# Routing by the graph's chunks of 125 rows, five of them added and normalised beside the last half hop

## What is computed

```python
    xn = _layernorm(x, axis=-1)
    x = x + _L0_gnn_ref(xn, ...) + _L0_mix_ref(xn[None], ...)[0]
    x = x + _L0_ffn_ref(_layernorm(x, axis=-1)[None], ...)[0]
    xn = _layernorm(x, axis=-1)
    x = x + _L1_gnn_ref(xn, ...) + _L1_mix_ref(xn[None], ...)[0]
    x = x + _L1_ffn_ref(_layernorm(x, axis=-1)[None], ...)[0]
```

```python
        for kk in range(NUM_K):
            gnn_out = gnn_out + _graph_gcn(gnn_out, row, col, gate_w[kk], gate_b[kk], n_nodes)
        return jnp.concatenate([x1, gnn_out], axis=1)
```

```python
        router_logits = jnp.einsum('bsh,he->bse', x, gate)
        routing_weights, selected = jax.lax.top_k(router_logits, TOP_K)
        routing_weights = jax.nn.softmax(routing_weights, axis=-1)
        ...
        out = jnp.einsum('ebsh,bse->bsh', eo, tok_w)
```

## Time and profile before

| | |
|---|---|
| median of 3 runs | 2486.34 us (2482.85 to 2488.85) |
| the profiled execution | 2485.95 us |
| its span (first to last instruction) | 2484.2 us |
| mean granted clock of TensorE | 0.945 |
| busy: TensorE / its weight loads / VectorE | 91% / 80% / 63% |
| busy: ScalarE / POOL | 40% / 10% |

### The profile page before, as it was taken

The page is one execution under the profiler, slowest core; times in us unless marked ns, Lnnn a source line. Parts: engine busy times, 40 slices in busy tenths (PEclk is TensorE's granted clock), DMA queues, the critical chain, the costliest instruction groups (busy, mean ns, idle before and its releaser), DMA issues. The chain is left out here.

```text
span 2484.2 us, 33706 instructions
## 1 busy us (share of the span) xinstructions
PE 2249.1 (91%) x12632; PEld 1984.6 (80%) x12632; DVE 1575.5 (63%) x2626; ACT 997.1 (40%) x1552; POOL 252.2 (10%) x262
## 2 busy tenths in 40 slices
PE   6889999996977999966999999958989999989898
PEld 4679999995866778765888888847789999978697
DVE  7646665568867888765899999957623333245422
ACT  4122232226744454413888888851121212221120
POOL 0057773000000000011000000011000000000000
PEclk9989999998997999956999999979999999999899
DMA  4332221114438345076445645134312111224314
GB/s 171 121 90 43 48 70 40 39 47 146 155 124 317 121 197 212 21 281 247 153 153 190 234 175 182 60 144 163 112 45 74 39 39 41 83 96 146 110 44 140
DMA packets 117152, 305.10 MB, mean 123 GB/s; under 512 B 18794, under 2 KB 45794, under 8 KB 116986
## 3 DMA queue, kind: packets, MB, share of 16 engines
q1 hardware_dynamic: 106170, 281.93, 32.0%
q0 software_dynamic: 10816, 20.99, 3.0%
HBM read 297.82 MB, written 126.51 MB: 171 GB/s over the span
## 5 line engine op out<-in xcount | busy, mean ns | idle before, releaser
L2255 DVE TENSOR_TENSOR ex_wl<-exraw,ex_wh 128x1024 fp32r<-128x1024 f32 x324 | 375.6, 1218 | 21.2 <-ACT ex_wh L2322 20.5
L2322 ACT ACTIVATE ex_wh<-exraw 128x1024 fp32r<-128x1024 f32 x324 | 328.5, 1057 | 49.3 <-DMA exraw<-in_experts 18.5
L1517 DVE TENSOR_TENSOR m_kvf<-m_bank,m_bkv 128x256 f32<-128x256 f32 (+1 forms) x160 | 67.9, 424 | 221.4 <-PE m_bank L1422 221.4
L1183 POOL DMA_INDIRECT scratch_slots<-pay,idx x160 | 197.8, 1236 | 57.5 <-issue 57.5
L1422 PE MATMUL m_bank<-m_w_lo,xh 128*128 128x256 f32 (+1 forms) x1280 | 178.3, 281 | 0.0
L1422 PE MATMUL m_bank<-m_w_hi,xl 128*128 128x256 f32 (+1 forms) x1280 | 177.0, 280 | 0.0
L1422 PE MATMUL m_bank<-m_w_hi,xh 128*128 128x256 f32 (+1 forms) x1280 | 176.9, 281 | 0.0
L1691 PE MATMUL gl_bank<-gl_gh,gl_al 125*125 125x512 f32 x400 | 159.1, 398 | 8.0 <-DVE gl_al L1859 8.0
L1422 PEld LDWEIGHTS m_bank<-m_w_lo,xh 128*128 128x128 f32 (+1 forms) x1280 | 163.9, 186 | 0.1
L1422 PEld LDWEIGHTS m_bank<-m_w_hi,xl 128*128 128x128 f32 (+1 forms) x1280 | 162.3, 186 | 0.0
L1422 PEld LDWEIGHTS m_bank<-m_w_hi,xh 128*128 128x128 f32 (+1 forms) x1280 | 161.4, 186 | 0.0
(11 more groups left out here) (437 smaller groups left out, 5159.4 us busy)
## 6 DMA issues: line engine op xcount, KB each, us to landing
exraw<-in_experts SPq DMA_DIRECT2D x328, 512.0 KB
scratch_seats<-raw SPq DMA_DIRECT2D x95, 512.0 KB
raw<-in_qkv SPq DMA_DIRECT2D x48, 512.0 KB, 5.6
xr<-scratch_res SPq DMA_DIRECT2D x42, 512.0 KB, 3.6
scratch_res<-xr SPq DMA_DIRECT2D x40, 512.0 KB, 3.9
xr<-scratch_seats SPq DMA_DIRECT2D x27, 512.0 KB, 3.7
scratch_served<-ex_y SPq DMA_DIRECT2D x27, 512.0 KB, 2.6
scratch_at<-xr SPq DMA_DIRECT2D x48, 209.0 KB, 1.9
```

Source lines behind the costliest of these rows:

```text
L1183: e.indirect_dma_start(dram["slot_rows"], bass.IndirectOffsetOnAxis(idx[:, k:k + 1].bitcast(U32), 0), pay[:, k, :], None).then_inc(scat.se ...
L1517: e.tensor_tensor(f, bank[KVB + s % 3][0:r, 0:W2], bkv[0:r], ALU.add)
L2255: return e.tensor_tensor(wl[:, n % RING], raw[:, unit[1]], wh[:, n % RING].bitcast(F32), ALU.subtract)
L2322: e.activation(wh[:, n % RING], raw[:, unit[1]], ACT.Copy).then_inc(high.sem)
```

## The change

- **Hops.** `graph_layer` gets the residual and its chunks' buffers (`rows`, `xn`). In the second hop SyncE loads eight chunks of 125 residual rows. The last half hop has no dots, bias, halving and spreads. VectorE takes in their place three `moments_of` (the addition of `g` to the residual's upper half, and moments) at steps 3, 5 and 7, two more and all five scalings after the loop. TensorE does the last `JOINT` = 3 steps bank by bank, so that the banks end one after another (`ended`). SyncE stores the five early chunks' sums to `res` and loads the residual's chunks 8 and 9 behind the first two. `x2` is gone: the result stays in `g`. `half` shares memory with `th` and `af`.
- **Routing** works on the ten chunks of 125. The first five come normalised; the last five are added and normalised here. The gate is SyncE's first transfer, the experts' four first units follow. On TensorE the order is turn(c+1), a ranking where c+1 is 5, 6, 7 or 9, scoring(c). `valid` and some memsets are gone. `Norm` takes its chunks, its rows and its depth of buffers.
- **Serving** works on the chunks of 125 too; its loads and stores go through `move`, two transfers each in place of one. The experts' unit buffers `exraw` are a list, half of which (`last`) lives from the graph's phase on.

```diff
+    def __init__(self, p, chunks=range(TC), rows=rows_of, depth=2):
...
+    HOPS, HALF, RING, LATE, JOINT = 4, TC // 2, 4, 2, 3
...
+        EARLY = T[:HALF]
+        norm = Norm(p, EARLY, node_rows, HALF)
+        x_in = [p.raises(f"x_in{c}", [c], 32) for c in T]
...
+        thaf = p.sb("thaf", [P, 6, HALF * TP])
+        th, af = thaf[:, 0:2], thaf[:, 2:6]
+        half = flat(thaf[:]).bitcast(U16)[:, 0:HALF * N].rearrange("p (c n) -> p c n", n=N)
...
+                if k == 1:
+                    for t in res_stored:
+                        e.wait_ge(*t.last())
+                    for c in T[:2 * HALF - 2]:
+                        move(e, rows[c], res[nodes(c)], x_in[c].sem)
                 for i in blanks[k * len(blanks) // HOPS:(k + 1) * len(blanks) // HOPS]:
                     e.dma_start(seats[i * P:(i + 1) * P], zero).then_inc(blanked.sem, 16)
             e.wait_ge(*blanked[blanks[-1]])
-            e.wait_ge(*rest_out[HOPS - 1, 1])
-            for c in T[:HALF]:
-                move(e, dram["x2"][nodes(c)], g[:, c], stored[c].sem)
-            for c in T[HALF:]:
-                e.wait_ge(*last_out[c])
-                move(e, dram["x2"][nodes(c)], g[:, c], stored[c].sem)
+            for c in EARLY:
+                e.wait_ge(*added[c])
+                move(e, res[nodes(c)], rows[c], x_out[c].sem)
+                if c == 2:
+                    for f, l in ((0, TC - 2), (1, TC - 1)):
+                        e.wait_ge(*x_out[f][f])
+                        e.wait_ge(*scaled[f])
+                        move(e, rows[l], res[nodes(l)], x_in[l].sem)
...
+                    joint = T[-JOINT:] if (k, h) == halves[-1] else T[TC:]
+                    for c in T[:TC - len(joint)]:
...
+                    for d in range(HALF) if joint else ():
+                        for c in joint:
+                            if d == 0:
+                                e.wait_ge(*a_low[k, h, c])
+                            b, cut = nth[k, h, c] % RING, slice(d * TP, d * TP + TP)
+                            o = bank[BANKS[h][d]][0:TP, :]
+                            e.matmul(o, al[0:TP, b, cut], gh[0:TP, c], start=False, stop=False)
+                            e.matmul(o, ah[0:TP, b, cut], gl[0:TP, c], start=False, stop=False)
+                            m = e.matmul(o, ah[0:TP, b, cut], gh[0:TP, c], start=False, stop=c == TC - 1)
+                        m.then_inc(ended.sem)
...
+                    if (k, h) != halves[-1]:
+                        copy_row(1 - h, (k, 1 - h))
+            for c in EARLY:
+                norm.root(e, c)
...
+            def moments_of(c):
+                t = rows[c][0:TP, NH:D]
+                e.wait_ge(*x_in[c][c])
+                e.tensor_tensor(t, t, g[0:TP, c], ALU.add).then_inc(added.sem)
+                e.drain()
+                norm.moments_of(e, rows[c][0:TP], c)
+
+            def scale(c):
+                norm.scale(e, xn[c][0:TP], rows[c][0:TP], c).then_inc(scaled.sem)
...
+                elif (k, half) == (0, halves[-1]):
+                    if s in (LATE + 1, LATE + 3, LATE + 5):
+                        moments_of((s - LATE - 1) // 2)
...
-            e.wait_ge(*a_done[HOPS - 1, 1, TC - 1])
+            moments_of(3)
+            scale(0)
+            moments_of(4)
+            scale(1)
             for d in range(HALF):
-                update(1, [d]).then_inc(last_out.sem)
-
-        p.hand_on(*stored)
-    return stored
+                e.wait_ge(*ended[d])
+                update(1, [d])
+                if d + 2 < HALF:
+                    scale(d + 2)
+
+        p.hand_on(*x_in[HALF:], *x_out)
+    return x_in[HALF:], x_out
...
-            def load(c):
-                if c >= BUFS:
-                    e.wait_ge(*x_out[c % BUFS][c - BUFS])
-                    e.wait_ge(*normed[c - BUFS])
-                e.dma_start(row(c), res[tokens(c)]).then_inc(x_in[c % BUFS].sem, 16)
-                for b in range(TC):
-                    if c * P < (b + 1) * TP and b * TP < c * P + rows_of(c):
-                        e.wait_ge(*x2_stored[b][b])
-                e.dma_start(xg[0:rows_of(c), c % BUFS], x2[tokens(c)]).then_inc(x_in[c % BUFS].sem, 16)
...
-            for c in range(BUFS):
-                load(c)
-                if c == 1:
-                    e.dma_start(flat(gr[:]), gate_dram).then_inc(ld.sem, 16)
-            for c in C:
+            e.dma_start(flat(gr[:]), gate_dram).then_inc(ld.sem, 16)
+            for u in range(FIRST):
+                e.dma_start(exraw[u], w_dram[u]).then_inc(units_in.sem, 16)
+            for c in C[H:]:
                 e.wait_ge(*added[c])
-                e.dma_start(res[tokens(c)], row(c)).then_inc(x_out[c % BUFS].sem, 16)
-                if c + BUFS < TC:
-                    load(c + BUFS)
-                else:
-                    for u in range(c - BUFS, min(c - BUFS + 1, FIRST)):
-                        e.dma_start(exraw[:, u], w_dram[u]).then_inc(units_in.sem, 16)
-            for b in range(KEPT, BUFS):
-                e.wait_ge(*x_out[b][TC - BUFS + b])
+                move(e, res[nodes(c)], rows[c], x_out[c - H].sem)
...
             for c in C:
-                r = rows_of(c)
                 if c % 2 == 0:
                     e.wait_ge(*seated[c // 2])
                 for k in range(TOP):
-                    e.indirect_dma_start(seats, bass.IndirectOffsetOnAxis(seat[0:r, k, c:c + 1].bitcast(U32), 0),
-                                         xn[0:r, c], None).then_inc(scattered.sem, 16)
+                    e.indirect_dma_start(seats, bass.IndirectOffsetOnAxis(seat[:, k, c:c + 1].bitcast(U32), 0),
+                                         xn(c), None).then_inc(scattered.sem, 16)
             e.wait_ge(*scattered[TC - 1, TOP - 1])
...
+                if c >= H:
+                    e.wait_ge(*normed[c])
...
-                if c >= 3 and c % 2:
-                    rank(c // 2 - 1)
+                b = c % 2
                 if c + 1 < TC:
                     turn(c + 1)
+                if c + 1 in (H, H + 1, H + 2, H + 4):
+                    rank((0, 1, 2, 3, 3)[c + 1 - H])
...
+                e.wait_ge(*x_in[c - H][c])
+                t = rows[c][0:TP, NH:D]
+                e.tensor_tensor(t, t, g[0:TP, c], ALU.add).then_inc(added.sem)
                 d()
...
-                    e.tensor_tensor(sel[:, pair], sel[:, pair], valid[:, pair].unsqueeze(2).broadcast_to([P, 2, EX]),
-                                    ALU.mult).then_inc(chosen.sem)
+                e.tensor_tensor(sel[:, pair], hot[:, 0, pair], hot[:, 1, pair], ALU.add).then_inc(chosen.sem)
...
-            moments_of(0)
-            for c in C:
-                r = rows_of(c)
+            moments_of(H)
+            for c in C[H:]:
                 if c + 1 < TC:
                     moments_of(c + 1)
-                n.scale(e, xn[0:r, c], row(c), c).then_inc(normed.sem)
-                if c >= 3 and c % 2:
-                    choose(c // 2 - 1)
-                if c >= 4 and c % 2 == 0:
-                    give(c // 2 - 2)
+                n.scale(e, xn(c), rows[c][0:TP], c).then_inc(normed.sem)
+                if c > H and c + 1 < TC:
+                    give(c - H - 1)
+                if c + 2 < TC:
+                    choose(c - H)
+            choose(PAIRS[-2])
...
-                e.dma_start(xr[0:rows_of(c), c % 3], res[tokens(c)]).then_inc(x_in[c % 3].sem, 16)
+                move(e, xr[:, c % 3], res[nodes(c)], x_in[c % 3].sem)
...
-                e.dma_start(res[tokens(c)], xr[0:rows_of(c), c % 3]).then_inc(x_out[c % 3].sem, 16)
+                move(e, res[nodes(c)], xr[:, c % 3], x_out[c % 3].sem)
...
+            with sb("g", [P, TC, NH]) as g, sb("exlast", [P, UNITS - FIRST, D]) as last:
+                rows = [xr[:, 0], xr[:, 1], xr[:, 2], raw[:, 1], raw[:, 2], last[:, 5], last[:, 6], last[:, 7],
+                        xr[:, 0], xr[:, 1]]
+                early = [last[:, c] for c in range(TC // 2)]
...
+                with sb("exfirst", [P, FIRST, D]) as begin:
+                    exraw = [begin[:, u] for u in range(FIRST)] + [last[:, u] for u in range(UNITS - FIRST)]
```

More of the change, by code:

```diff
@@ L1592, in graph_layer @@
         blank, blanked = p.raises("blank", ["zero"]), p.raises("blanked", blanks, 16)
[L1593 to L1594 removed]
+        EARLY = T[:HALF]
+        norm = Norm(p, EARLY, node_rows, HALF)
+        x_in = [p.raises(f"x_in{c}", [c], 32) for c in T]
+        added, scaled, x_out = p.raises("added", EARLY), p.raises("scaled", EARLY), [p.raises(f"x_out{c}", [c], 32) for c in EARLY]
+        p.take(*res_stored)
         gh, gl = p.sb("gh", [P, TC, NH], F32R), p.sb("gl", [P, TC, NH], F32R)
@@ L1887, with route @@
 FIRST = 4
-def route(nc, tag, x2, res, gate_dram, seats, seat, answer, share, plan, x2_stored, res_stored, xr, w_dram, exraw):
+def route(nc, tag, g, res, gate_dram, seats, seat, answer, share, plan, rows, early, x_in, w_dram, exraw):
     with Phase(nc, tag) as p:
-        C, U = range(TC), range(KC)
```

(37 more changed lines are left out.)

181 lines of the change are left out of this document (79 added, 102 removed).

## The result

The changed kernel takes 2499.76 us (median of 5 runs, 2494.92 to 2504.17), the kernel before 2487.46 (5 runs, 2482.85 to 2489.11): a ratio of 1.005, 95% interval 1.0031 to 1.007. It is **slower by 0.5%**, where 2475.7 us and a faster kernel were forecast; the time lies above the stated range of 2468 to 2483. On another chip it was 1.004 (1.0024 to 1.0056).

What follows compares the result with a forecast made beforehand. Phases add up; TensorE bounds routing, and VectorE would end the graph's phase. The terms -13.9 - 0.2 + 0.4 + 1.9 + 1.2 = -10.6 us take 2485.95 to 2475.3, median 2475.7; range 2468 to 2483.

Steps and rivals of the forecast that it cites:

- The bound and the first part of the sum: Graph's end through routing: VectorE ends the graph's phase, TensorE bounds routing; last choice at 1120.5 instead of 1134.4, 13.9 us gained.
- First turn: Start of routing: the gate, now issued first, lands after 3.0 us, so TensorE's first turn comes at 1062.5.
- Ten turns, scorings and rankings: TensorE in routing: ten turns, ten scorings and four rankings take 57.6 us, plus 0.4 before the last choice.
- The three moments in the loop: Graph's last half hop: three moments, 8.2 us, lie inside VectorE's loop, which it leaves at 1042.0 instead of 1042.1.
- Scatters and gathers of 125 rows: Routing's end and serving's start: slower landings add 0.4 us at the last scatter and 1.9 before the first mixing.
- The second case: Five engines, in turn: 125-row transfers use five engines, three fly at once; 1.8 us over the forecast, 2477.5; chance 0.32.
- the third case: Scatters always on the same five engines can't overlap, taking 81 us; about 2513, slower than before; chance 0.04.
- Small items: Serving: a second store issue 0.4, 27 more rows 0.2, waits and semaphore clears 0.6, together +1.2 us.
- the clock rises: Routing: TensorE's work halves at a higher clock, VectorE sets the pace, the time is 2454; chance 0.08.
- A clock above 0.50: Routing: turns and scorings were expected without gaps at granted clock 0.50; a higher clock would show the forecast wrong.

Runs made afterwards that it cites:

- sc120: The changed kernel with scatters of 120 rows, five rows of each chunk not brought to the experts, gathers as they were: 2483.13 us, run once.
- pad_no_joint_2: Second run of the kernel padded to 128 rows with the last three steps' products step by step and updates behind the last product: 2475.36 us.
- pad_sc127: The changed kernel with gathers padded to 128 rows but scatters of 127 rows: 2583.04 us, one run on a slower chip.
- pad_both: The padded kernel: the changed kernel with every scatter and gather padded from 125 to 128 rows: 2472.78 us, ratio 0.9949 to the kernel before.
- pad_uncut: The kernel padded to 128 rows, with serving's residual loads as one 128-row transfer instead of 112 + 13: 2468.65 us, ratio 0.994 to the kernel before.

## Why the prediction was wrong, point by point

- **The bound and the first part of the sum: right.** Forecast: a graph's phase of 323.0 us (736.5 to 1059.5); measured 322.8. VectorE, not TensorE, ends it, 4 us behind the last product, and undoing the bank order costs what that says. First turn: forecast 3.0 us behind routing's start, measured 1.7. Ten turns, scorings and rankings: forecast 58.0 us, measured 55.8 with the clock up for a moment and 58.7 or 58.8 in two traces (`sc120`, `pad_no_joint_2`) where it stayed at 0.50; in the third such trace, `pad_sc127`, it was 60.1. Together 17.6 us gained up to the last choice, 13.9 forecast, and some 3 of the 17.6 are the clock's, which the forecast did not have. (The three moments in the loop stand at steps 5, 7 and 9 counted from 0, not at 3, 5 and 7; VectorE left the loop 305.2 us into the phase, 305.5 forecast.)
- **The step that failed: "Scatters and gathers of 125 rows".** It took the 98-row landing of the earlier trace rows as the measure, scaled its excess to 1.9 us, and charged +0.4 for the scatters' tail and +1.9 for the first gather. Measured: +13.4 and +9.7 against before, 23.1 us where 2.3 were forecast; 11.4 and 8.5 by the padded kernel on one chip. Of the sum's terms this one alone turned a gain into a loss: all the others together measured -13.3 against -12.9 forecast, and that they agree so well is luck, as a larger computing gain and 5.5 us of scatter ahead of the graph's phase offset what serving and the phases behind it lost. 98 divides by 14; no number from 6 to 16 divides 125. The nearest row in bytes was the wrong neighbour: it lay on the other side of the rule.
- **The second case had the mechanism and a wrong price.** "Five engines, in turn" forecast a landing of 6.3 us; the first scatter took 7.0. What failed is its next sentence, "three can fly at once". The second scatter is issued 1.54 us behind the first, but in the packet records nothing of it starts earlier than 3.9 us behind the first one's first packet (about 1.5 us with 128 rows). Later scatters do overlap, and not all on the same five engines: from 1120 to 1130 the queue moves 234 GB/s, nearly twice 5/16 of 404. Yet it is not 404, though the share is 0.92: a packet of 4096 bytes takes 0.249 us in the mean of the twenty scatters against 0.169 in `pad_both`, with medians of 0.159 and 0.162. So the landings grow from 7.0 to 18.0, and the last packet ends 17.7 us behind the last issue (3.7 in `pad_both`). The truth lies between the second and the third case. I had priced the second at 1.8 us over the forecast.
- **What the second and third case left out.** The landing of a single scatter on an idle queue does not tell what a queue costs that is fed faster than it drains. The rival that ended slower had the right question (does a scatter cost more than the interval between issues?) and I set its chance at 0.04.
- **Small items: +1.2 forecast.** Measured +6.2 in the rest of serving and +4.4 behind it. Of the first, 2.7 are the cut loads by `pad_uncut`'s one trace, which were priced as issues alone (and only the stores). The later gathers are not shown to cost anything: on one chip the changed kernel has 151.7 there and the padded one 152.0. Of the second, 1.2 stand in the second attention, whose first products run at 0.50 for longer (10.2 us at that level where it was 6.8); the kernels with the change have it in each trace. Another 2.1 stand in the gated MLP, which takes 134.9 to 137.9 us over all traces, so that part may be scatter. The rest I did not settle.
- **The partial clock.** The rival "the clock rises" was given 0.08 as all or nothing. It rose for some us in nine of the twelve traces that have the change, and was worth about 3 in most. A clock above 0.50 stood among the signs of being wrong; it came, and helped.

## What to carry to other kernels

Before an indirect transfer is given a new row count, factor the count: padding 125 rows to 128 bought 20 us of 2490 here, at the cost of three wasted rows. When the change is a sum of a computing gain and a transfer that "lands a little later", ask whether the queue still drains faster than it is fed; the price of one transfer alone does not tell. And take as the measure of a row count one with a like divisor, not one with a like number of bytes.

## What the runs showed that I had not expected

- 124 rows on four engines cost hardly more than 125 on five (32.4 against 30.8 and 27.6 us, first landing 6.8 against 7.0), while 127 rows on one engine cost 110.0. Why the queue's rate at 125 rows is 234 GB/s at a share of 0.92, and not in proportion to the engines, is open. The packet records say that the rows' packets took longer in the mean (0.249 against 0.169 us), and not why; nor is it shown why the second scatter starts late.
- POOL's issue of a scatter grows with the packets: 0.96 us with 128 rows (144 packets), 0.98 with 126 (160), 1.18 with 125 (416), 2.54 with 127 (2048); with 127 rows it stands still for 32.20 us after seven issues and for 29.20 after fourteen.
- A granted clock of 1.0 for some us in the middle of an unbroken run of TensorE work, in some traces and not in others of the same kernel.
